# A GRU scan feeding a mixture of experts: the first transfers issued in another order, two input blocks turned later, spare products ahead of the first state part

## The reference, cut to what matters

```python
def cell(h, x):                       # 128 steps in the source's T; here x is (16, 256, 512): 256 steps
    gi = x @ W_ih + b_ih              # W_ih, W_hh: 512 x 1536
    gh = h @ W_hh + b_hh
    i_r, i_z, i_n = jnp.split(gi, 3, axis=-1)
    h_r, h_z, h_n = jnp.split(gh, 3, axis=-1)
    r = jax.nn.sigmoid(i_r + h_r)
    z = jax.nn.sigmoid(i_z + h_z)
    n = jnp.tanh(i_n + r * h_n)
    return (1.0 - z) * n + z * h

_, hs = jax.lax.scan(cell, cond_2048, x by time)     # h is 16 x 512
# then for each of the 4096 rows of hs: 8 experts of rank 128, the best 2 of them weighted
norm = max(||row||, 1e-12)
rw, chosen = top_k(softmax(row / norm @ router_w), 2);  rw = rw / sum(rw)
combine = sum(one_hot(chosen) * rw)
out = x + sum_e combine[:, e] * (row @ Wa[e] @ Wb[e])
```

## Time and profile before

| | |
|---|---|
| median of 3 runs | 1015.8 us (1015.31 to 1016.97) |
| the profiled execution | 1016.61 us, of which the profile's span is 1014.8 us |
| TensorE, granted clock over the span | 0.998 |
| busy share of the span: PE, DVE, ACT, POOL | 97%, 86%, 69%, 29% |
| start of the first GRU step on VectorE (L737) | 27.25 us from the span's start |
| its second and third | 30.96 us, 34.69 us |

### The profile page before, as it was taken

The page is one execution under the profiler, slowest core; times in us unless marked ns, Lnnn a source line. Parts: engine busy times, 40 slices in busy tenths (PEclk is TensorE's granted clock), DMA queues, the critical chain, the costliest instruction groups (busy, mean ns, idle before and its releaser), DMA issues.

```text
span 1014.8 us, 60727 instructions
## 1 busy us (share of the span) xinstructions
PE 979.8 (97%) x29067; PEld 669.7 (66%) x20799; DVE 877.1 (86%) x3637; ACT 695.7 (69%) x2696; POOL 292.5 (29%) x723
## 2 busy tenths in 40 slices
PE   4789999999999999999999999999999999999997
PEld 2456666666666667766666666666676677676674
DVE  6889888888888888888888888888888888888887
ACT  6687766776766776666677676677666667766664
POOL 1032233232333332323332332332332332233223
PEclk9999999999999999999999999999999999999999
DMA  8321111111111111111111111101111101110000
GB/s 294 94 81 30 30 32 30 26 31 31 28 32 30 28 29 33 27 32 33 28 26 35 27 31 30 32 24 34 30 29 30 33 23 34 30 30 20 14 9 28
DMA packets 49360, 38.83 MB, mean 38 GB/s; under 512 B 34532, under 2 KB 38972, under 8 KB 49084
## 3 DMA queue, kind: packets, MB, share of 16 engines
q1 hardware_dynamic: 48236, 31.41, 11.5%
q10 hardware_dynamic: 848, 3.54, 1.1%
HBM read 18.94 MB, written 8.39 MB: 27 GB/s over the span
## 4 chain that ended last, share of the span: by engine, by line
PE 90%; DVE 5%; DMA 2%; ACT 1%; issue 1%; SPq 0%; POOL 0%; DVEq 0%; POOLq 0%
PE pairs L872 16%; PE ybank L872 12%; PE gates L952 11%; PE gates L957 11%; PE pairs L863 8%; PE ybank L863 6%; PE zbank L872 5%; PE zbank L863 5%; PE obank L872 5%; PE nbank L872 5%; PE obank L863 3%; PE nbank L863 2%; DMA whh<-in_L_cond_W_hh 1%; DVE tr L737 1%; DVE acc L820 1%
## 5 line engine op out<-in xcount | busy, mean ns | idle before, releaser
L872 PE MATMUL pairs<-wx,xs 128*32 128x384 f16 x4096 | 280.8, 327 | 1.5 <-DVE wx L717 1.4
L599 ACT ACTIVATE rr<-pre 128x64 f32<-128x64 f32 x256 | 65.9, 258 | 239.8 <-DVE pre L740 239.8
L872 PE MATMUL ybank<-hparts,wa 128*128 128x128 f16 x2048 | 194.0, 219 | 0.0
L461 POOL TENSOR_TENSOR y<-y 128x128 f16<-128x128 f32 x256 | 106.4, 436 | 256.5 <-ACT y L650 251.9
L872 PEld LDWEIGHTS ybank<-hparts,wa 128*128 128x128 f16 x2048 | 159.9, 98 | 29.8 <-issue 16.7
L863 PE MATMUL ybank<-hparts,wa 128*128 128x128 f16 x1024 | 178.3, 219 | 0.0
L863 PE MATMUL pairs<-wx,xs 128*32 128x384 f16 x2048 | 174.1, 326 | 0.0
L952 PE MATMUL gates<-whh,st 128*32 128x256 f16 x4080 | 157.3, 273 | 15.4 <-DVE st L768 15.0
L872 PEld LDWEIGHTS pairs<-wx,xs 128*32 128x32 f16 x4096 | 108.3, 96 | 95.9 <-issue 54.1
L952 PEld LDWEIGHTS gates<-whh,st 128*32 128x32 f16 x4080 | 103.5, 96 | 84.7 <-ACT gates L571 62.6
L957 PE MATMUL gates<-whh,hparts 128*32 128x256 f16 x4080 | 157.5, 273 | 0.0
(11 more groups left out here) (138 smaller groups left out, 1820.9 us busy)
## 6 DMA issues: line engine op xcount, KB each, us to landing
out<-outb SPq DMA_DIRECT2D x63, 128.0 KB
xin<-in_x SPq DMA_DIRECT2D x58, 128.0 KB
wih<-in_L_cond_W_ih ACTq DMA_DIRECT2D x4, 768.0 KB, 7.9
whh<-in_L_cond_W_hh SPq DMA_DIRECT2D x4, 768.0 KB, 11.9
wih<-in_L_ffn_Wb SPq DMA_DIRECT2D x8, 256.0 KB, 2.6
xs<-xh SPq DMA_TRANSPOSE x116, 3.0
wih<-in_L_ffn_Wa SPq DMA_DIRECT2D x4, 256.0 KB, 5.0
whh<-in_L_ffn_Wa SPq DMA_DIRECT2D x4, 256.0 KB, 2.9
```

Source lines behind the costliest of these rows:

```text
L461: nc.gpsimd.tensor_tensor(y[:, m % YB, 1, :], y32[:, m % 2, :], y[:, m % YB, 0, :], ALU.subtract).then_inc(ylo_ready, 1)
L599: nc.scalar.activation(rr[:, :], pre[:, RG, :, :].rearrange("p k b -> p (k b)"), ACT.Sigmoid, scale=1 / PROD_SCALE).then_inc(r_ready, 1)
L872: return nc.tensor.matmul(out, lhsT, rhs, start=start, stop=stop, skip_group_check=True)
```

## The change

Five edits.

1. ScalarE issues no weights and no block 0 at its beginning. SyncE issues, without a wait at its head, the four quarters of W_ih, block 0, the four quarters of W_hh, the router's weights, and blocks 1 and 2, these no longer behind a wait.
2. ScalarE issues the three bias transfers behind its first small activation, and the four of the starting state behind piece 2.
3. Block 0 is split, and the starting state turned, behind piece 11 (before: piece 8).
4. Block 1 is turned in step 0 (before: ahead of the first state part) and block 2 in step 1 (before: step 0); their splits are in steps 0 and 1 on ScalarE and in steps 1 and 2 on VectorE (before: ahead of step 0 and in step 0; in steps 0 and 1).
5. Ahead of each quarter of the first state part, but not of the last one, and behind the quarter's wait, TensorE does four spare products of 128 x 384 into a bank that nobody reads.

```diff
@@ SyncE
-            sp.wait_ge(consts_ready, 2)
-            groups = "(g j c) -> j g c"
-            sp.dma_start(bias_h[0:P:32, HN, :], b_hh[2 * D:3 * D].rearrange("(j c) -> j c", j=K)).then_inc(bias_loaded, 16)
-            sp.dma_start(bias_h[0:P:32, RG:ZG + 1, :], b_hh[0:2 * D].rearrange(groups, g=2, j=K)).then_inc(bias_loaded, 16)
-            sp.dma_start(bias_i[0:P:32, :, :], b_ih.rearrange(groups, g=3, j=K)).then_inc(bias_loaded, 16)
-            for j in range(K):
-                sp.dma_start(cond_sb[32 * j:32 * j + B, :], cond[:, j * P:(j + 1) * P]).then_inc(cond_loaded, 16)
+            def load_ih(k):
+                sp.dma_start(wih32[:, k, :, :].rearrange("p g n -> p (g n)"), W_ih[k * P:(k + 1) * P, :]
+                             ).then_inc(wih_loaded[k], 16)
+
+            for k in range(K):
+                load_ih(k)
+            load_first(0)
             for k in range(K):
                 load_hh(k)
             sp.dma_start(rw32[:, :, :], router_w.rearrange("(p k) e -> p k e", k=K)).then_inc(rw_loaded, 16)
             for b in (1, 2):
-                sp.wait_ge(whh_loaded[b], 16)
                 load_first(b)
@@ ScalarE, its beginning
-            for k in range(K):
-                if k == 2:
-                    act.dma_start(xin[:, 0, :], x_blocks[0]).then_inc(first_loaded[0], 16)
-                act.dma_start(wih32[:, k, :, :].rearrange("p g n -> p (g n)"), W_ih[k * P:(k + 1) * P, :]
-                              ).then_inc(wih_loaded[k], 16)
@@ ScalarE, beside(n)
-                if n == 0:
-                    split_first(2)
+                if n + 1 < FIRST:
+                    split_first(n + 1)
@@ ScalarE, before step 0
             nc.scalar.activation(table_use[:, :], ones[:, :], ACT.Sigmoid)
+            load_biases()          # the three bias transfers, behind wait_ge(consts_ready, 2)
             for n in range(N_GRU_SPLITS):
                 split_weights(n)
-                if n == 8:
+                if n == 2:
+                    load_cond()    # the four transfers of the starting state
+                if n == N_IH_SPLITS - 1:
                     split_first(0)
                 if n == N_IH_SPLITS:
                     keep_biases()
...
-            split_first(1)
@@ VectorE, beside(n)
-                if n < FIRST - 1:
-                    split_first(n + 1)
+                if 1 <= n < FIRST:
+                    split_first(n)
@@ TensorE
+            def keep_busy():
+
+                for _ in range(BUSY):          # BUSY = 4
+                    nc.tensor.matmul(nbank[:, 0:3 * P], wx[:, 0, 0, 0, 0:P], wx[:, 0, 0, 0, :], start=True, stop=True,
+                                     skip_group_check=True)
...
                             pe.wait_ge(weights_split, splits_before(N_IH_SPLITS + 3 * (k + 1)))
+                        if pw == 0 or k + 1 < K:
+                            keep_busy()
                         for bank, cols, done in sides:
@@ TensorE, wide_step(n)
                 pair_ahead(n)
+                if n == 1:
+                    turn_first(2)
@@ TensorE, grouped_step(n)
                 if n == 0:
-                    turn_first(2)
+                    turn_first(1)
@@ TensorE, before step 0
             pair_part(1, range(6))
-            turn_first(1)
             first_state_part()
```

More of the change, by code:

```diff
@@ L43, in gru_moe_kernel @@
     AHEAD = 3
+    BUSY = 4
     FIRST = 3
@@ L539, in _, with load_biases, load_cond @@
         def _(act):
-            for k in range(K):
-                if k == 2:
-                    act.dma_start(xin[:, 0, :], x_blocks[0]).then_inc(first_loaded[0], 16)
-                act.dma_start(wih32[:, k, :, :].rearrange("p g n -> p (g n)"), W_ih[k * P:(k + 1) * P, :]
-                              ).then_inc(wih_loaded[k], 16)
+            groups = "(g j c) -> j g c"
+            def load_biases():
+                act.wait_ge(consts_ready, 2)
+                act.dma_start(bias_h[0:P:32, HN, :], b_hh[2 * D:3 * D].rearrange("(j c) -> j c", j=K)).then_inc(bias_loaded, 16)
+                act.dma_start(bias_h[0:P:32, RG:ZG + 1, :], b_hh[0:2 * D].rearrange(groups, g=2, j=K)).then_inc(bias_loaded, 16)
+                act.dma_start(bias_i[0:P:32, :, :], b_ih.rearrange(groups, g=3, j=K)).then_inc(bias_loaded, 16)
+            def load_cond():
+                for j in range(K):
+                    act.dma_start(cond_sb[32 * j:32 * j + B, :], cond[:, j * P:(j + 1) * P]).then_inc(cond_loaded, 16)
             def split_weights(n):
```

## The result

The changed kernel takes 1022.12 us (median of 6 runs, 1020.66 to 1022.72) against 1015.75: ratio 1.0059, 95% interval 1.0049 to 1.0070. Run once more beside the experiments it took 1021.71, ratio 1.0056 (1.0043 to 1.0070). The forecast was 1019.0, +3.2 us; the change is +6.0 us by the ratio and +6.4 by the medians. By the two profiled executions the span grew from 1014.8 to 1020.3, 5.5 us; the executions themselves by 5.7. The other 0.6 us to the medians is that the profiled execution of before lay 0.8 over its median and the one of after 0.2.

What follows compares the result with a forecast made beforehand. TensorE is busy throughout the middle, so only the start can move: first step 2.7 us later plus 0.55 in step 2 make 3.2 on the median 1015.8, 1019.0. Forecast +2.0 to +4.3 us (0.62); range 1016.8 to 1021.2.

Steps and rivals of the forecast that it cites:

- all other steps as they were: Scan: expected sign that only the third step after the first transpose lengthens, by 0.5 us, and no other step changes.
- C: Start: half pace over all bias products (+1.8) or small transfers behind SyncE's (+4), 1021 to 1023; 0.12 with another rival.
- D: Last quarters of first state part: array at half pace despite spare products, 2.6 + 0.9 more, 1022.5; 0.12 with another rival.
- Block 0 later, and all that hangs on it: Start: TensorE begins at 13.9, not 10.08; bias products end at 19.1, last high piece at 26.2, 1.35 us later.
- +1.8 and -1.3: TensorE up to the first pair's input products: how far this term might be off, in us, through half or full pace.
- Spare products: Behind the last high piece: 16 later ones cost 2.6 us, net 2.0 in the sum; 12 earlier ones are off the path.
- a group of four 0.66; that price is certain to a few per cent at full pace: TensorE, first state part: four full-array spare products of 384 columns take 0.66 us, at 0.165 each.
- Block 2's split in step 2: VectorE, step 2: the moved split delays step 3's transpose by 0.55 us, bounds 0 and 0.65.
- a difference that changes after the fourth step: Scan: one of the signs by which the forecast would be wrong; no size given.
- A: Start: block 0 lands sooner, at 12.3 in place of 13.9; +1.6 us, 1017.4, no change that can be told; chance 0.20.
- B: Start: ScalarE goes at the weights' pace, bias products done by 16; 1015.8, no change; chance 0.06.

Runs made afterwards that it cites:

- e9_block0_spread: The changed kernel with input block 0 issued as eight transfers of 32 KB in place of one of 256 KB: 1022.18 us, ratio 1.0055.
- e7_spares_waited: The changed kernel with spare products only ahead of the high part's first three quarters (12 of the 28): 1019.53 us, ratio 1.0031.
- e2_block0_second: The changed kernel with block 0 issued between the second and third quarter of W_ih: 1019.68 us, ratio 1.0035.
- e8_quarter_spares: The changed kernel with each spare product of 128 columns of weights replaced by four of 32 columns: 1020.7 us, ratio 1.0046.
- e4_old_transfers: The kernel before plus the later turns and splits of blocks 1 and 2 and the spare products, transfers as before: 1019.18 us, ratio 1.0026.
- e5_split2_early: The changed kernel with both turns at the head of step 0, ScalarE's splits in step 0, VectorE's in steps 0 and 1: 1021.21 us, ratio 1.0052.
- e6_busy_step3: The changed kernel with one more group of four spare products behind step 3's input products: 1021.65 us, ratio 1.0052.
- e10_second_and_early: Changed kernel: block 0 second, its split and state's transpose behind piece 8, 32-column spares only at three waited-for quarters and in step 3: 1015.27 us, ratio 0.9995.
- e11_and_spread: Changed kernel: block 0 second in eight transfers, split and state's transpose behind piece 8, 32-column spares only at three waited-for quarters and step 3: 1014.74 us, 0.9988.
- e1_no_spares: The changed kernel without its 28 spare products: 1019.13 us, ratio 1.0025.
- e3_turns_alone: The kernel before with only block 1 turned in step 0, block 2 in step 1, and their splits moved as in the change: 1016.66 us, ratio 1.0005.
- e12_changed_again: The changed kernel, unaltered, run once more on the same chip beside other experiments: 1021.71 us, ratio 1.0056.

## Why the forecast missed: right way, wrong size

The sum was 3.2 us and the two profiles end 5.46 apart. Of the missing 2.3 us 1.05 are the fall of the clock behind step 3, which the forecast put at nothing with the words "all other steps as they were": this is the step that failed. 0.67 are the tail behind the last high piece, 0.45 block 0 and what hangs on it, 0.16 step 12; step 3 itself was 0.09 less than forecast. That the median of 1022.1 lies where the rivals C (1021 to 1023) and D (1022.5) had put the time is chance: neither mechanism made it.

- **Block 0 later, and all that hangs on it: right.** 13.9 forecast, 14.18 measured; bias products 19.1 and 19.68; the last high piece 26.2 and 26.65. Moving the one issue back gave 2.06 us. The 0.45 too little is 0.3 of block 0's arrival and 0.13 of a slightly longer half pace (5.40 us from the first transpose to the input products, before 5.27), inside the stated +1.8 and -1.3.
- **Spare products: the term that was mis-sized.** The step "a group of four 0.66; that price is certain to a few per cent at full pace", with 0.18 for the quarter, gave 3.75 us from the last high piece to the first step (26.2 to 29.95); it took 4.42 (26.65 to 31.07). The surplus is 0.2 us a group for the change between 128-column and 32-column weights, and goes with it (1.03 and 0.82). The earlier trace rows had the pace inside one shape only. The Trainium skill, TensorEngine Tiling (Array Packing), "Key Properties", says in one line that changing the tiling mode drains TensorE; it gives no price, and the forecast did not weigh it. The two profiles agree with it, 1.03 against 0.82 us, and in the changed kernel the weights after a change of shape start to load only with their products; that a drain is the cause they do not show. Net the 16 late ones cost 2.67 where I had 2.0.
- **Block 2's split in step 2: right.** 0.55 forecast, 0.46 to 0.47 in every profile that has it.
- **Missing: the clock in the steps.** I weighed a fall ahead of the first step alone (rival D) and wrote "all other steps as they were". The delay in step 2 also lengthens TensorE's wait, to 2.18 us, and in most executions of the changed kernel the clock falls behind it, 1.05 us more. By the mean clock this fall is in 10 of the 11 executions of the changed kernel, in 4 of 5 of `e9_block0_spread`, 5 of 9 of `e7_spares_waited`, 2 of 5 each of `e2_block0_second` and `e8_quarter_spares`, and 1 of 8 of `e4_old_transfers`. In none of the 32 executions of the four kernels whose profiles have a shorter wait there is one: 1.73 us in `e5_split2_early`, 1.42 in `e6_busy_step3`, 1.53 in `e10_second_and_early` and `e11_and_spread`. So the longer wait is needed, but it is not enough: with the same 2.18 us the clock did not fall there in the profiles of `e1_no_spares`, `e2_block0_second`, `e3_turns_alone` and `e7_spares_waited`. What decides between one execution and the next no run here shows. The forecast's own sign of being wrong, a difference that changes after the fourth step, did come.
- **Rivals.** A did not happen. B, no slower kernel, would have needed block 0 early. C's longer half pace cost the changed kernel's profile 0.13 us and not 1.8; it came in other profiles, where the same work took 6.30 us (`e6_busy_step3`) and 6.37 (`e1_no_spares`) in place of 5.40. C's other half, small transfers stuck behind SyncE's, did not happen. D did not happen: the spare products kept the pace.
- **The ends of the range.** 2.7 + 0.55 = 3.2 became 3.82 + 0.46 + 1.05 + 0.16. The first two terms alone, 4.3, are at the very edge of the forecast's own +4.3; the third goes past it and, with the fourth, past the end of the whole range too (1021.2, +5.4). The two executions with no fall, at 1020.11 (`e9_block0_spread`) and 1020.66 (the changed kernel), lie inside it. The range gave the clock in the steps no room.
- **Open:** the 0.16 in step 12. It is in the profiles with the new transfers (0.15 in `e10_second_and_early` and `e12_changed_again`) and not in `e4_old_transfers`. The timeline of ScalarE has its place: `wt` (L648), which stands ahead of the z gate, starts 0.55 us behind `rr` and not 0.28, idle for 0.30 with GpSimd's `top_no` (L480) as the releaser. But GpSimd's instructions lie at the same distance from the step's opening as before, so why ScalarE waits is not known.

## What to carry to other kernels

Look for the transfer that starts the longest serial chain before giving each matrix its place by the order of its use: here a small block held four bias products, and these held the row of weight splits, for 2.06 us. Work that only keeps a clock up belongs where the engine waits anyway, in the shape of its neighbours; behind the last wait it is on the path in full. Even in the right place it may bring nothing that the median shows, as here. And a delay of half a microsecond on another engine can cost three times that if it stretches a wait of TensorE.

## What the runs showed that was not expected

- Going between 128-column and 32-column weights cost TensorE 0.1 us each way: 1.03 us against 0.82 for the same columns streamed.
- From the first product after a long wait, the half pace lasted less than 3.5 us in the profile of before (from 10.08; the second pair of L912, at 13.60, is at full pace) and over 5 in others (`e6_busy_step3`: from 14.00, and the second pair of L920, 17.86 to 19.57, is at half pace throughout). The second bias pair then takes 1.86 to 1.91 us in place of 1.02, though TensorE's work up to there is the same: 0.7 to 0.9 us between executions. The runs of one kernel with no fall in the steps differ by as much (1020.9 and 1022.4 in `e6_busy_step3`); that this is the reason is likely and not shown, for each has one profile.
- The same wait of 2.18 us is followed by a fall of the clock in some executions and not in others: 1018.2 against 1019.5 to 1020.3 for one kernel.
- 256 KB of the input take 2.3 us of the transfers' time, and what runs beside them slows with them to 225 GB/s, from 420, at a full busy share. Eight transfers in place of one bring 256 to 307 and the weights behind them 0.8 to 0.9 us sooner, the block itself only 0.2.
- One small instruction of GpSimd took 0.40, 0.74 and 2.55 us in three kernels (`hist` from the turned state), and in the last ScalarE waited for it.
